# Image rows of three channels interleaved over the partitions in the patch embedding of a vision tower

## The chip, the cores and the metric

The kernel runs on one core of a Trainium2 chip. The metric is the device time of one execution in microseconds (us). It is given as the median of several executions, and one more execution was recorded by the hardware profiler.

## The reference, cut to what matters

The input is 128 images of three channels with 224 x 224 float32 pixels. Each image is cut into 8 x 8 patches of 28 x 28 pixels. A patch, with its three channels, is a vector of 3 * 28 * 28 = 2352 numbers, and a weight of 128 x 2352 turns it into a token of 128 numbers:

```python
patches = X.reshape(B, C, N_PATCHES, PATCH, N_PATCHES, PATCH)
patches = patches.transpose(0, 2, 4, 1, 3, 5).reshape(B, N_PATCHES * N_PATCHES, IN_D)
tokens = jnp.einsum('bpi,hi->bph', patches, W) + b
```

A class token goes in front (65 tokens per image), and all are multiplied by position factors. Then come a gated attention block with a damped moving average over each image position's 128 images, its layer norms, and a mixture of 8 experts of which each takes the 1024 tokens with the highest router scores, works on them, and adds its weighted result into the output. All of it is float32.

## The kernel before, in words

Names: B = 128 images, C = 3 channels, PATCH = 28, NP = 8 patches per row of patches, ROWS = C * PATCH = 84, EXTRA = 42, KROWS = 126, PASSES = 19, CHUNK = 16 images, RING = 3.

**Loading.** The images are loaded in 64 chunks. Chunk n holds, for 16 images, the 28 pixel rows of one row of patches, in all three channels. It goes into one of three ring buffers `RAW` with pixel rows on the partitions: `load_chunk` (L418) issues on the SP queue one DMA per channel, 28 partitions x 16 images x 224 pixels (896 bytes in one piece). In the kernel before, `raw` puts channel c on the partitions 28c to 28c + 27, so that the row p of channel c stands on partition 28c + p. `stage_W` on SP issues the load of chunk n + 3 when chunk n has left its ring buffer.

**Spreading.** The sum over 2352 products is made as 19 passes of a matmul over up to 126 partitions: a pass takes one pixel column q of the patch on the partitions 0 to 83, and for the last REST = 9 columns the pixel rows are also put on the partitions 84 to 125, so that two passes share the work of one more column. ScalarE copies the first 19 columns of each chunk out of the ring buffer (`stage_C` on ACT, L794, three pieces). GpSimd copies the other 9 columns into a staging tile `ST` (`stage_C` on POOL, L563), and two DMAs on its own queue (`stage_w`, L576, here called the extras) bring the partitions 0 to 41 and 42 to 83 of it to the partitions 84 to 125 of the operand.

**Weights.** The weight `WN`, 128 outputs x 2352, is put by three copies on VectorE (L863 to L865) into `WP`, which has for each pass t the 126 or 84 weights in the order in which the pixel rows stand on the partitions. TensorE transposes it (L1315 to L1319) and ScalarE brings it to `WT`.

**Order of the work.** One list, `SLOT`, sets for all engines the order of the stages within half a row of patches: "C k piece", "w k" and "W k" are the copy, the extras and the next load of chunk k of four, and the other letters are the stages of two groups of four tokens each, the newer (a) and the older (b). Every engine runs its own stages in this order. TensorE puts the token passes (`token_pass`, L1333) between the stages. A pass of a half row begins once all four of its chunks have been copied and their extras have landed. The group's matmul L1399 (stage D) comes once in each half row and waits for ScalarE's L710 (stage F), which in ScalarE's order stands behind copies of chunks. In the iteration for i = 0 there is only the class token's small group; the full groups begin in the iteration for i = 1.

After the last token pass the last groups are finished, the experts' tokens are chosen, gathered, worked on and scattered. The change does not touch that part.

Of the kernel before, what the change touches and what calls it, by code (L numbers as in the profile page):

```python
# [35 lines left out]
def vit_tower(nc, x, tok_w, tok_b, cls_token, pos_embed, proj_v_w, proj_v_b, proj_mx_w, proj_mx_b,  # L36
# [10 lines left out]
    B, C, IMG, _ = x.shape  # L47
    SEQ, D = pos_embed.shape
    NP = 8
    PATCH = IMG // NP  # L50
# [3 lines left out]
    HEADS = damping.shape[1]  # L54
    MAXPOS = (rel_pos_w.shape[0] + 1) // 2
    E, _, FF = w1.shape
    FC = FF // 128
    CAP = 1024
# [14 lines left out]
    ROWS = C * PATCH  # L73
    EXTRA = ROWS // 2
    KROWS = ROWS + EXTRA
    REST = 9
    PASSES = PATCH - REST
    HALF = B // 2
    NCOL = HALF * NP
    CHUNK = 16  # L80
# [5 lines left out]
    RING = 3  # L86

    ctx = ExitStack()
    with ctx:
# [13 lines left out]
        RAW = flat[:, 2 * PLANEW + STAGEW:2 * PLANEW + STAGEW + RING * RAWW].rearrange("p (a n) -> p a n", a=RING)  # L103
# [50 lines left out]
        WN = slab1[:, 0:C * PATCH * PATCH]  # L154
        WP = slab1[:, 2352:2352 + PASSES * 128].rearrange("p (t k) -> p t k", t=PASSES)
# [193 lines left out]
        def group(row, u):  # L349
            g = 2 * row + 1 + u  # L350
            return Group(row, g, u, 4, 4 * g - 3, 1 - u)
# [30 lines left out]
        def run(eng, stages, tokens_at=None, last=True):  # L382

            def iteration(i, slots, tokens, more):
                for u, (a, b) in enumerate(slots):
                    for s, w in slot(i, u, a, b, tokens, more):
                        if s in stages:
                            stages[s](*w)
                        if tokens_at and tokens and s not in "KCWw":
                            tokens_at(s, i, a, u)  # L390
                    if tokens_at and tokens:
                        tokens_at("end", i, a, u)

            def pair(i):
                return (group(i - 1, 0), group(i - 2, 1)), (group(i - 1, 1), group(i - 1, 0))
            iteration(0, ((CLS, None), (None, None)), True, True)
            iteration(1, ((group(0, 0), CLS), (group(0, 1), group(0, 0))), True, True)
            for i in range(2, NP - 1):
                iteration(i, pair(i), True, True)
            iteration(NP - 1, pair(NP - 1), True, False)  # L400
            if last:
                iteration(NP, pair(NP), False, False)
                iteration(NP, ((None, group(NP - 1, 1)),), False, False)


        @block.sync
        def _(sp):
            def rows_of(k, hy, c):
                return x[CHUNK * k:CHUNK * k + CHUNK, c, ds(hy * PATCH, PATCH), :].rearrange("b p w -> p b w")

            def raw(n, c):
                return RAW[PATCH * c:PATCH * c + PATCH, n % RING, :].rearrange("p (b w) -> p b w", b=CHUNK)

            def load_chunk(n):

                if n < CHUNKS * NP:
                    for c in range(C):
                        sp.dma_start(raw(n, c), rows_of(n % CHUNKS, n // CHUNKS, c)).then_inc(load[n % RING].sem, 16)  # L418

            def stage_W(k, hy):  # L420

                n = CHUNKS * hy + k
                sp.wait_ge(*copied.done(n))
                sp.wait_ge(*staged.done(n))
                sp.sem_inc(passed_sp.sem, 1)
                load_chunk(n + RING)

            load_chunk(0)
            sp.dma_start(WN, tok_w).then_inc(w_loaded.sem, 16)
            for n in range(1, RING):  # L430
                load_chunk(n)
            for k in range(4):
                stage_W(k, 0)

            def stage_M(gr):
                sp.wait_ge(*dve_M.done(gr.g, 3))
                sp.dma_start(out[:, ds(gr.position, gr.tiles), :], O[:, 0:gr.tiles, :]).then_inc(out_stored.sem, 16)

            def stage_R(gr):
                sp.wait_ge(*dve_Q.done(gr.g))  # L440
                sp.sem_inc(passed_sp.sem, 1)
                sp.dma_start(rows_v[:, ds(gr.position, gr.tiles), 0:D], XR[:, 0:gr.tiles, :]).then_inc(row_stored.sem, 16)

            run(sp, {"W": stage_W, "M": stage_M, "R": stage_R}, last=False)


            def load_experts(h, e):
                sp.dma_start(W1s[:, h, :], w1[ds(e, 1), :, :].rearrange("e d f -> d (e f)")).then_inc(w_in[h].sem, 16)
                sp.dma_start(W2s[:, h, :, :], w2[ds(e, 1), :, :].rearrange("e (c f) d -> f (e c) d", f=128))\
                    .then_inc(w_in[h].sem, 16)  # L450

            sp.wait_ge(*pe_tok[0].done(NP - 1))
            sp.wait_ge(*pe_tok[1].done(NP - 1))
            for h in range(2):
                load_experts(h, h)
            for gr in (group(NP - 2, 1), group(NP - 1, 0), group(NP - 1, 1)):
                stage_M(gr)
                stage_R(gr)


            sp.wait_ge(*pr_ready.done(0))
            sp.dma_start(rows_v[:, :, D:ROW], PR).then_inc(pr_stored.sem, 16)

            for e in range(1, E - 1):
                sp.wait_ge(*pe_y.done(2 * e - 1))
                load_experts(1 - e % 2, e + 1)

            sp.wait_ge(*out_stored.done(LAST))
            sp.wait_ge(*row_stored.done(LAST))
            sp.wait_ge(*pr_stored.done(0))  # L470
# [379 lines left out]
        def _(dve):  # L850
# [8 lines left out]

            dve.wait_ge(*c_loaded.done(0))  # L860
            dve.wait_ge(*w_loaded.done(0))
            wn = WN.rearrange("p (k q) -> p q k", q=PATCH)
            dve.tensor_copy(WP[:, :, 0:ROWS], wn[:, 0:PASSES, :])  # L863
            dve.tensor_copy(WP[:, 0:REST, ROWS:KROWS], wn[:, PASSES:PATCH, 0:EXTRA])
            last = dve.tensor_copy(WP[:, REST:2 * REST, ROWS:KROWS], wn[:, PASSES:PATCH, EXTRA:ROWS])  # L865
            last.then_inc(wp_ready.sem, 1)


# [236 lines left out]
            for it in range(STEPS):  # L1105
                k = it % 7
# [5 lines left out]
                for j in range(2):  # L1112
                    last = dve.tensor_scalar(seen[0:KEYS, j, :], keys[0:KEYS, :], CA[:, j:j + 1], 0.0, ALU.is_lt, ALU.add,
                                             accum_out=cnt[0:KEYS, j:j + 1])
# [497 lines left out]
```

## Time and profile before

| | us |
|---|---|
| median of 3 executions | 1035.58 |
| lowest and highest | 1031.78, 1038.38 |
| the profiled execution, its own time | 1028.54 |
| its span in the trace | 1026.8 |

The trace counts from the span's start. PE is TensorE's matmul, PEld its weight load, DVE is VectorE, ACT is ScalarE, POOL is GpSimd, SP is the engine that only issues DMAs; SPq is its queue. A group of instructions is named by its line and by what it writes and reads; XS is the large tile that holds ring buffers, staging tile and operand alike. "DMA share" is the mean busy share of the core's 16 DMA engines.

### The profile page before, as it was taken

The page shows a single profiled execution, that of the slowest core. Times are in us where ns is not written, and L with a number is a line of the kernel's source. Part 1 is how long each engine was busy: PE and PEld are TensorE (multiplying, and loading weights), DVE is VectorE, ACT ScalarE, POOL GpSimd, SP SyncE. Part 2 cuts the span into 40 slices and gives each one's busy share as a digit, 9 for nine tenths or more (in the row PEclk, how much of TensorE's full clock was granted, in tenths as well). Part 3 has the DMA queues.
Part 4 walks back from the last instruction along what each step waited for, and adds up shares of the span by engine and source line. Part 5 has one row for each costly group of instructions (what it writes and reads, how often), then busy time and mean ns, then how long its engine had stood idle before and what let it go on. Part 6 is the DMA issues. An engine that isn't in the chain of part 4 may idle for free.

```text
span 1026.8 us, 9698 instructions
## 1 busy us (share of the span) xinstructions
PE 739.8 (72%) x2872; PEld 396.3 (39%) x2872; DVE 552.4 (54%) x1238; ACT 446.5 (43%) x729; POOL 474.5 (46%) x486
## 2 busy tenths in 40 slices
PE   0268379979998999999989995625214599996740
PEld 0123135435444544554445454404113455553310
DVE  0210156676778578877876777692687534321110
ACT  0634346647656656665666532321261233322200
POOL 2232344454545445554554422261200658888775
PEclk9778789989999999999999997866555699988875
DMA  9799999998999999999999301000010123444332
GB/s 218 145 190 190 183 189 183 186 196 179 201 183 190 204 202 194 204 211 204 177 204 201 82 21 42 20 11 11 21 11 1 45 57 60 81 63 66 36 32 25
DMA packets 135648, 126.31 MB, mean 123 GB/s; under 512 B 17589, under 2 KB 125997, under 8 KB 135469
## 3 DMA queue, kind: packets, MB, share of 16 engines
q1 hardware_dynamic: 113600, 91.27, 43.5%
q0 software_dynamic: 19456, 33.44, 18.0%
q10 hardware_dynamic: 2540, 0.99, 0.5%
q8 instruction: 23, 0.38, 0.2%
q14 instruction: 29, 0.23, 0.1%
HBM read 87.92 MB, written 12.98 MB: 98 GB/s over the span
## 4 chain that ended last, share of the span: by engine, by line
PE 30%; DMA 22%; POOL 15%; DVE 11%; issue 9%; ACT 7%; SPq 3%; ACTq 1%; POOLq 0%; DVEq 0%
DMA XS<-in_x 18%; PE bank L1333 12%; POOL out L617 9%; POOL XS L606 4%; ACT XS L794 3%; SPq L418 3%; ACT XS L812 2%; PE bank L1399 2%; DVE XR L892 2%; PE bank L1431 2%; PE bank L1416 2%; PE bank L1462 2%; PE bank L1402 1%; DVE Y L950 1%; DMA out<-XS 1%
## 5 line engine op out<-in xcount | busy, mean ns | idle before, releaser
L1333 PE MATMUL bank<-XS,WT 126*128 126x512 f32 (+1 forms) x608 | 314.2, 653 | 38.3 <-DMA XS<-XS 38.3
L794 ACT ACTIVATE XS<-XS 84x1152 f32<-84x1152 f32 (+1 forms) x192 | 188.9, 1027 | 71.0 <-DMA XS<-in_x 69.6
L1333 PEld LDWEIGHTS bank<-XS,WT 126*128 126x128 f32 (+1 forms) x608 | 113.9, 196 | 175.9 <-issue 175.1
L563 POOL COPY XS<-XS 84x1152 f32<-84x1152 f32 x64 | 89.3, 1395 | 104.1 <-DMA XS<-in_x 100.5
L617 POOL DMA_INDIRECT out<-XS x64 | 101.3, 1583 | 24.8 <-issue 18.6
L606 POOL DMA_INDIRECT XS<-token_rows,XS x64 | 65.2, 1019 | 77.2 <-issue 65.4
L576 POOL DMA_DIRECT2D XS<-XS x128 | 71.4, 560 | 63.2 <-PE bank L1333 48.3
L950 DVE TENSOR_TENSOR_SCAN Y<-qdec,XT 128x512 f32<-128x512 f32 (+1 forms) x68 | 77.4, 1159 | 7.5 <-ACT XT L681 7.5
L837 ACT ACTIVATE XS<-bank,VT 128x512 f32<-128x512 f32 x64 | 44.0, 687 | 65.5 <-PE bank L1539 65.5
L1539 PE MATMUL bank<-XS 128*128 128x512 f32 x128 | 66.3, 666 | 1.1 <-ACT XS L681 0.8
L956 DVE SCALAR_TENSOR_TENSOR ET<-Y,ema_c,ET 128x512 f32<-128x512 f32 (+1 forms) x68 | 63.5, 933 | 1.8
L1549 PE MATMUL bank<-XS 128*128 128x512 f32 x128 | 57.5, 592 | 0.0
L1399 PE MATMUL bank<-ET,WmT 128*128 128x512 f32 (+1 forms) x34 | 23.7, 786 | 42.5 <-ACT ET L710 42.4
L539 POOL TENSOR_TENSOR QT<-QT,XT 128x512 f32<-128x512 f32 (+1 forms) x17 | 23.6, 1391 | 61.1 <-ACT QT L762 61.1
L912 DVE SCALAR_TENSOR_TENSOR tokT<-bank,VT 128x512 f32<-128x512 f32 x16 | 17.7, 1109 | 61.3 <-PE bank L1333 61.3
L681 ACT ACTIVATE XS<-bank 128x512 f32<-128x512 f32 x16 | 9.6, 597 | 83.1 <-PE bank L1530 83.1
L1243 DVE TENSOR_SCALAR XS<-bank,VT 128x512 f32<-128x512 f32 x16 | 12.0, 749 | 62.1 <-PE bank L1549 62.1
L892 DVE TENSOR_SCALAR XR<-O,mvC,rsC 128x128 f32<-128x128 f32 x65 | 38.5, 855 | 12.4 <-POOL rsC L489 12.4
L487 POOL TENSOR_SCALAR rsB<-mvB 128x4 f32<-128x4 f32 (+1 forms) x17 | 15.1, 889 | 61.2 <-DVE mvB L905 61.2
L1011 DVE SCALAR_TENSOR_TENSOR G<-bank,VT,GT 128x512 f32<-128x512 f32 (+1 forms) x34 | 24.5, 727 | 33.8 <-PE bank L1431 33.3
L986 DVE TENSOR_TENSOR S<-bank,relb 128x512 f32<-128x512 f32 (+1 forms) x17 | 11.3, 667 | 57.3 <-PE bank L1416 57.3
L1253 DVE TENSOR_TENSOR XS<-bank,XS 128x512 f32<-128x512 f32 x16 | 11.1, 692 | 53.3 <-DMA out<-XS 46.5
(229 smaller groups left out, 1293.2 us busy)
## 6 DMA issues: line engine op xcount, KB each, us to landing
XS<-in_x SPq DMA_DIRECT2D x192, 392.0 KB
XS<-XS POOLq DMA_DIRECT2D x128, 189.0 KB, 8.8
out<-O SPq DMA_DIRECT2D x16, 256.0 KB, 10.9
token_rows<-XR SPq DMA_DIRECT2D x16, 256.0 KB, 12.4
XS<-in_L_ffn_W SPq DMA_DIRECT2D x16, 256.0 KB, 3.2
XS<-in_L_tok_W SPq DMA_DIRECT2D x1, 1176.0 KB, 10.3
XS<-token_rows,XS POOLq DMA_INDIRECT x64
out<-XS POOLq DMA_INDIRECT x64
```

The costliest lines, as they stand in the source:

```text
L563: pool.tensor_copy(ST[0:ROWS, n % 2, :, :, :].rearrange("p m j r -> p m r j"), px[:, :, :, PASSES:PATCH])\
L576: pool.dma_start(area(slice(ROWS, KROWS), k // 4, a, m0, m0 + CCOL // 2), ST[EXTRA * a:EXTRA * a + EXTRA, n % 2, :, :, :]).then_inc(extras ...
L606: pool.indirect_dma_start(out=XG[h][:, k, :], out_offset=None, in_=rows_d, in_offset=bass.IndirectOffsetOnAxis(ap=IDX[:, e, k:k + 1], axis ...
L617: pool.indirect_dma_start(out=out_flat, in_=OW[:, e % 2, k, :], in_offset=None, out_offset=bass.IndirectOffsetOnAxis(ap=IDX[:, e, k:k + 1] ...
L794: ins = act.activation(area(slice(0, ROWS), k // 4, piece, m0, m0 + CCOL // 2).rearrange("p m j r -> p m r j"), px[:, :, :, REST * piece:m ...
L892: last = dve.tensor_scalar(dst(t), src(t), mv[:, gr.parity, t, 0:1], rs[:, gr.parity, t:t + 1], ALU.subtract, ALU.mult)
L950: dve.tensor_tensor_scan(Y[:, h % 2, 0:n], qdec[:, h, 0:n], XT[:, p, 0:n], 0.0, ALU.mult, ALU.add)\
L956: dve.scalar_tensor_tensor(out=ET[:, gr.parity, 0:n], in0=Y[:, h % 2, 0:n], scalar=ema_c[:, h:h + 1], in1=ET[:, gr.parity, 0:n], op0=ALU.m ...
L1333: ins = pe.matmul(TOK[half][:, :], WT[rows, t, :], area(rows, half, t // REST)[:, :, t % REST, :], start=(t == 0), stop=(t == PASSES - 1))
L1399: pe.matmul(DB0[:, 0:n], WmT[:, 1, :], et, start=True, stop=True).then_inc(pe_D.sem, 1)
L1539: pe.matmul(bank[3 + f][:, :], W1s[:, h, 128 * f:128 * f + 128], XGT[:, half, :], start=True, stop=True).then_inc(pe_hid.sem, 1)
L1549: last = pe.matmul(bank[7][:, :], W2s[:, h, f, :], HT[:, half, f, :], start=(f == 0), stop=(f == FC - 1))
```

## The change

The rows of the three channels are interleaved over the partitions: row p of channel c stands on partition 3p + c in place of 28c + p. Each load DMA still has 28 partitions, but they are three apart and reach from c to c + 81. The three weight copies write the weights in the same order. The staging tile, the extras, the copies out of the ring and the matmuls keep their shapes and partitions; what they hold is in another order.

```diff
             def raw(n, c):
-                return RAW[PATCH * c:PATCH * c + PATCH, n % RING, :].rearrange("p (b w) -> p b w", b=CHUNK)
+                return RAW[c:ROWS:C, n % RING, :].rearrange("p (b w) -> p b w", b=CHUNK)
...
             dve.wait_ge(*w_loaded.done(0))
-            wn = WN.rearrange("p (k q) -> p q k", q=PATCH)
-            dve.tensor_copy(WP[:, :, 0:ROWS], wn[:, 0:PASSES, :])
-            dve.tensor_copy(WP[:, 0:REST, ROWS:KROWS], wn[:, PASSES:PATCH, 0:EXTRA])
-            last = dve.tensor_copy(WP[:, REST:2 * REST, ROWS:KROWS], wn[:, PASSES:PATCH, EXTRA:ROWS])
+            wn = WN.rearrange("o (c p q) -> o q p c", c=C, q=PATCH)
+            part = PATCH // 2
+
+            def rows(t0, t1, k0, k1):
+                return WP[:, t0:t1, k0:k1].rearrange("o t (p c) -> o t p c", c=C)
+
+            dve.tensor_copy(rows(0, PASSES, 0, ROWS), wn[:, 0:PASSES, :, :])
+            dve.tensor_copy(rows(0, REST, ROWS, KROWS), wn[:, PASSES:PATCH, 0:part, :])
+            last = dve.tensor_copy(rows(REST, 2 * REST, ROWS, KROWS), wn[:, PASSES:PATCH, part:PATCH, :])
             last.then_inc(wp_ready.sem, 1)
```

## Rows read from the trace of the kernel before

**Rows 1.** The page's part 2, DMA: busy tenths and GB/s in 40 slices.

```profile
DMA  9799999998999999999999301000010123444332
GB/s 218 145 190 190 183 189 183 186 196 179 201 183 190 204 202 194 204 211 204 177 204 201 82 21 42 20 11 11 21 11 1 45 57 60 81 63 66 36 32 25
```

**Rows 2.** The page's part 6, DMA issues, count and size of one.

```profile
XS<-in_x SPq DMA_DIRECT2D x192, 392.0 KB
XS<-XS POOLq DMA_DIRECT2D x128, 189.0 KB, 8.8
out<-O SPq DMA_DIRECT2D x16, 256.0 KB, 10.9
```

**Rows 3.** Timeline of POOL: the staging copy of chunks 2, 3, 4, 11, 15.

```profile
30.31 1.29 POOL L563 COPY XS<-XS 84x1152 f32<-84x1152 f32 x1 [4.69 <-DMA XS<-in_x]
46.83 1.28 POOL L563 COPY XS<-XS 84x1152 f32<-84x1152 f32 x1 [13.17 <-DMA XS<-in_x]
53.03 1.29 POOL L563 COPY XS<-XS 84x1152 f32<-84x1152 f32 x1 [3.62 <-issue]
...
112.91 1.28 POOL L563 COPY XS<-XS 84x1152 f32<-84x1152 f32 x1 [5.84 <-DMA XS<-in_x]
...
146.85 1.29 POOL L563 COPY XS<-XS 84x1152 f32<-84x1152 f32 x1 [2.38 <-DMA XS<-in_x]
```

**Rows 4.** The chain that ended last, three of its pieces from 27 to 150 us.

```profile
14.91 12.75 DMA lnb<-in_L_attn_ln_b
...
39.10 7.48 DMA XS<-in_x
...
114.98 9.64 DMA XS<-XS
```

**Rows 5.** Timeline of PE: the group's matmul L1399, one per half row.

```profile
149.66 2.07 PE L1399 MATMUL bank<-ET,WmT 128*128 128x512 f32 x2 [5.86 <-ACT ET L710]
...
401.22 1.13 PE L1399 MATMUL bank<-ET,WmT 128*128 128x512 f32 x2 [1.49 <-ACT ET L710]
434.60 1.13 PE L1399 MATMUL bank<-ET,WmT 128*128 128x512 f32 x2 [0.40 <-ACT ET L710]
```

**Rows 6.** The chain again, L1399 of the last loading half row and of the next.

```profile
574.46 1.12 PE bank L1399 x2
...
606.63 1.13 PE bank L1399 x2
```

**Rows 7.** The table of waits, from 190 to 580 us.

```profile
ACT XS L794 <- DMA XS<-in_x: 25.8, 12, 6.9
```

**Rows 8.** Timeline, all engines: a chunk copy that waits, and L710 behind it.

```profile
398.17 2.50 ACT L794 ACTIVATE XS<-XS 84x1152 f32<-84x1152 f32 x2 [2.24 <-DMA XS<-in_x]
...
400.55 0.62 ACT L710 ACTIVATE ET<-ET 128x512 f32<-128x512 f32 x1
```

**Rows 9.** Busy time by stretch: the last two columns are DMA share and GB/s.

```profile
42.00:44.00 2.00, 0.00 (x0) 0.00 (x0) 0.00 (x0) 1.42 (x2) 0.00 (x0) 0.50 0.99 190
...
100.00:150.00 50.00, 28.21 (x75) 13.18 (x74) 16.77 (x38) 19.98 (x26) 20.29 (x26) 0.80 0.97 186
...
618.00:620.00 2.00, 0.75 (x7) 0.51 (x6) 1.61 (x4) 0.80 (x2) 0.00 (x0) 1.00 1.04 304
```

**Rows 10.** Timeline from 27 us: the three weight copies on DVE.

```profile
27.68 1.70 DVE L863 COPY XS<-XS 128x1596 f32<-128x1596 f32 x1 [27.68 <-DMA lnb<-in_L_attn_ln_b]
...
29.29 0.52 DVE L864 COPY XS<-XS 128x378 f32<-128x378 f32 x1
29.73 0.53 DVE L865 COPY XS<-XS 128x378 f32<-128x378 f32 x1
```

**Rows 11.** One line of the source, L418: the load DMAs as issued on SP.

```profile
L418 SPq DMA_DIRECT2D XS<-in_x x192: 315/566/5013, 0.8 to 561.3; - x192
```

**Rows 12.** The table of waits, from 35 to 190 us.

```profile
POOL XS L563 <- DMA XS<-in_x: 67.8, 13, 13.2
...
PE bank L1333 <- DMA XS<-XS: 38.3, 3, 22.5
```

## The prediction, made before the changed kernel was run

> **What bounds the kernel now.** I read the page's slices first. The DMA engines are 90% busy or more in nearly every slice up to the 22nd (some 565 us), and they move 180 to 210 GB/s there; after that they are mostly idle [rows 1]. So the first 565 us look like a transfer-bound stage, and the last 450 us, from the last token pass on, have other limits and hold no image load. The sizes of the DMAs give the load of a chunk: three DMAs of 392 KB, which is 1.204 MB, and two extras of 189 KB, which is 0.387 MB, in all 1.591 MB [rows 2].
>
> The timeline of POOL confirms it for the ramp. Its staging copy starts as soon as a chunk has landed. Chunk 4 is staged at 53.03 us and chunk 15 at 146.85, so 11 chunks take 93.8 us, 8.53 us each [rows 3]. 1.591 MB in 8.53 us is 187 GB/s, and the stretch from 100 to 150 us shows 186 GB/s at a DMA share of 0.97 [rows 9]. Nothing but transfers sets the pace there. In the table of waits of that stretch POOL waits 67.8 us for the loads and TensorE 38.3 us for the extras [rows 12].
>
> From 150 us on full groups are in the pipeline, and another limit stands close by. The group's matmul L1399 comes once per half row. It stands at 149.66 us and, 12 half rows later, at 574.46 [rows 5, 6]: 424.8 us, 35.4 each. One of these periods, 401.22 to 434.60, is only 33.38 us with all four chunks in it [rows 5]. The first period with no load left, 574.46 to 606.63, is 32.17 us [rows 6]. So the groups' own chain of dependences needs 32 to 33.4 us, and only the rest is the transfers' fault. A typical case: a chunk copy on ScalarE waits 2.24 us for its load, and L710, for which L1399 waits, stands right behind it [rows 8]. From 190 to 580 us these waits are 25.8 us in total [rows 7].
>
> **The change part by part.**
>
> *The loads.* The number of DMAs, their bytes and their pieces of 896 bytes stay. Only the 28 partitions that one DMA writes change: neighbours before, every third one now. What pace can a load have? From 42 to 44 us almost nothing but loads of chunk 3 is under way: 190 GB/s at a DMA share of 0.99 [rows 9]. From 618 to 620 us the same 16 engines fetch expert weights from the same memory, onto all 128 partitions, and move 304 GB/s at 1.04 [rows 9]. So an engine that is called busy does not have the same pace in both; something holds the image loads. The chunk's 1.204 MB take 6.34 us at 190 GB/s, and would take 3.96 us at 304. The two ends are a saving of 0 and of 2.4 us per chunk; an end below zero is in the rivals. I take 243 GB/s, near the middle, since the 28 partitions are spread over the tile but are still 28 and not 128: 4.95 us, a saving of 1.4 us per chunk.
>
> The row shows 190 GB/s for a load onto 28 neighbouring partitions. The Trainium skill, page "SBUF — State Buffer", section "Door 1: The DMA port swizzle (why [64,N] ≈ [32,N])", says that DMA writes pass through 16 ports of 27.2 GB/s each, that four neighbouring partitions (and the four that lie 32 further) share one, and that a span's pace follows the ports it reaches. By that rule 28 neighbours reach 7 ports, 190 GB/s, and the trace agrees exactly. Three apart they reach 13 ports, and the fullest has 8 of a chunk's 84 rows instead of 4 of each DMA's 28; the page's estimate for the new loads would be 84/8 times 27.2 = 286 GB/s, 4.2 us per chunk.
>
> *Issue on SP.* 192 issues of 0.32 us at least, 0.57 in the median [rows 11]. Their number stays. I cost the stride of three at nothing; below the load's pace it is hidden as long as three issues stay under a chunk's period, about 7 us. The long ones, up to 5.01 us [rows 11], are issues that the full queue holds back; with a faster queue they shorten.
>
> *The weight copies.* Three copies of 1.70, 0.52 and 0.53 us, which lie on the path to the first chunk copy at 35.4 us [rows 10]. They read single elements far apart before and after, and write in rows before and after. I cost the new order at 0; the ends are -0.3 and +2.7 us, the latter if the longer stride doubled all three.
>
> *Extras, chunk copies, matmuls.* Same shapes on the same partitions: 0. The extras take 0.387 MB at 190 GB/s, 2.04 us of the engines per chunk. Their own pace may change by who writes beside them; for that see the rivals.
>
> **The sum**, against the profiled execution's own 1028.5 us:
>
> (a) Start. Chunk 3 is fetched alone, 7.48 us [rows 4]: -1.4. The constants land at 27.66 us behind three chunks [rows 4], which would need 4.2 us less; the constants themselves have a share in it, so I count half: -2. Together -3.4.
>
> (b) Chunks 3 to 11, staged at 46.83 and 112.91 us [rows 3], 8 intervals: 8 x 1.4 = -11.2. This goes through to TensorE, since the second iteration's first token pass waits for the extras of chunk 11, which land at 124.6 [rows 4].
>
> (c) Those extras, 9.64 us in a shorter queue [rows 4]: -1. Chunks 12 to 15 until L1399 at 149.66: 4 x 1.4 = -5.6, of which I count -5, as L1399 itself was idle for 5.86 us before it [rows 5]. Together -6.
>
> (d) The 12 half rows from 149.66 to 574.46. The engines would need, per half row, 4 x (4.95 + 2.04) = 28.0 us, and two stores of 256 KB [rows 2] at 190 GB/s, 2.8 us: 30.8 in all. That is below the 33.4 us of the groups' chain, which now becomes the bound: 12 x (35.4 - 33.4) = -24. This agrees with the 25.8 us of waits [rows 7]. If the transfers' waits vanish wholly, 32.2 us is the floor and the term is -38; if a wait of 1 us per half row stays, it is -12.
>
> (e) From 574 us on: 0. The groups, the choice of tokens and the experts run as before.
>
> Sum: -3.4 - 11.2 - 6 - 24 = -44.6, about -45. The profiled execution would have 984 us. It lies 7 us under the median of 1035.6; I take the same difference off the median: 990.6, rounded 990. After the change the transfers are late less often, and in the steady stage what is late next is VectorE's and TensorE's chain through a group.
>
> **The rivals.**
>
> *Nearly the full pace* (chance 0.20). Once no neighbours are written by one DMA, the loads come near the 304 GB/s of the weight load [rows 9]: at 285 GB/s a chunk takes 4.2 us, 2.1 less. The page's rule on ports, above, would have it so. Then (a) is -5, (b) is -17, (c) is -7.5 (the idle time in front of L1399 limits it) and (d), with 27 us of transfers under a chain of 32.2 to 33.4, some -30: -60 in all, 976 us. For it: all loads of a chunk are in flight together, so that their rows cover the tile more evenly than one DMA does. [...]
>
> *No change* (0.17). What holds the image loads is not where they are written but how they are read: pieces of 896 bytes from rows far apart, against long rows for the expert weights [rows 9]. Then every term is 0: 1036 us. For it: the rows of before cannot tell the two apart. Against it: the extras, which read no DRAM, share the stretch at the same 187 GB/s [rows 9], so the reading of short rows cannot be all of it. A part of the same doubt: the Trainium skill, page "DMA: Bandwidth & Descriptors", section "Why a DMA increments its semaphore by 16 and not by 1", has a DMA of 28 partitions use 14 engines at most, before and after. No row here shows single engines.
>
> *Only the ramp gains* (0.06). The loads are faster, but in the steady stage the order of the slots makes each load be asked for so late that the copies wait as before; (a) to (c) stay, (d) is 0: -20.6, 1015 us. Against it: 33.38 us was reached with loads under way [rows 5].
>
> *Slower* (0.06). The extras write the partitions 84 to 125. Before, two of three load DMAs (partitions 0 to 55) wrote far from them; now every load writes from the bottom up to partition 83. If that hinders the extras, their 2.04 us per chunk grow. It decides from the point at which they lose more than the loads' 1.4 us, at 1.7 times their time. At 2.5 times, 5.1 us, a chunk needs 8.38 + 3.06 - 1.4 = 10.0 us, a half row 42.9 with its stores, 7.5 more than now, over 12 half rows +90, and +20 in the ramp: 1145 us; at 2 times it is +0.6 us per chunk, over 64 chunks +40: 1075 us, which I take for it. Against it: TensorE waited for extras only three times, all in the ramp [rows 12], and loads and extras overlap already.
>
> **How the numbers follow.** The forecast itself has 0.51, the others 0.20, 0.17, 0.06, 0.06. The forecast's own range is 975 to 1005: (d) between -12 and -38, the load's saving between 1 and 1.8 us. The range for 8 in 10 goes from 965, where all ends on the good side come together (-70), to 1030, inside the case of no change. About 1% (10 us) is what a measurement of this kernel can tell from no change. Faster by more than that: the forecast, nearly the full pace, the ramp alone, 0.77 together. Within 1%: 0.17. Slower: 0.06.
>
> **What would show it.** Right: in the ramp chunks are staged some 7.1 us apart in place of 8.53, with over 210 GB/s; L1399 comes every 33 to 34 us; the waits of chunk copies for loads between 190 us and the last load fall from 25.8 us to under 6; the DMA share in the steady stage falls from 0.97 towards 0.9; the stage from the last loading half row on is as long as before. Wrong: 8.5 us and 187 GB/s as before (no change), or 6.4 us or less (nearly the full pace). Extras that land clearly later than 8.8 us after issue [rows 2] would speak for the slower case. An L863 of much over 1.7 us would put the weight copies right in the sum. The forecast as a whole falls if the loads get faster and L1399 still comes every 35 us.

## The result, and the profile after

The changed kernel has a median of 1003.23 us in four executions (1000.45 to 1005.40). The kernel before, run beside it once more, has 1033.68 us over four. The ratio of the two is 0.970, 95% interval 0.965 to 0.975: faster by 30 us. The forecast was 990 us with a gain of 45; the time lies inside the forecast's own range, 975 to 1005 us, near its upper end, and the gain is two thirds of what was foretold.

The page of the changed kernel, its span and the parts that answer to [rows 1, 2]:

```profile
span 1001.4 us, 9698 instructions
...
DMA  9699998898889888988986120000010223443332
GB/s 218 150 206 208 201 205 197 197 217 196 206 197 217 201 202 195 217 192 203 209 195 161 37 64 21 0 22 10 11 11 4 48 58 62 83 65 64 35 34 24
...
XS<-in_x SPq DMA_DIRECT2D x192, 392.0 KB
XS<-XS POOLq DMA_DIRECT2D x128, 189.0 KB, 7.7
out<-O SPq DMA_DIRECT2D x16, 256.0 KB, 6.9
```

The same bytes move at 192 to 217 GB/s in the full slices while the loads last, where it was 177 to 211, and the engines' digits fall from 9 to 8 in many slices: the transfers have room again. Extras land 7.7 us after their issue in place of 8.8, stores after 6.9 in place of 10.9.

The timeline of POOL, the staging copies of the chunks 3, 4, 11 and 15, as in [rows 3]:

```profile
46.70 1.29 POOL L563 COPY XS<-XS 84x1152 f32<-84x1152 f32 x1 [12.45 <-DMA XS<-in_x]
52.35 1.29 POOL L563 COPY XS<-XS 84x1152 f32<-84x1152 f32 x1 [3.06 <-issue]
...
107.30 1.28 POOL L563 COPY XS<-XS 84x1152 f32<-84x1152 f32 x1 [5.36 <-DMA XS<-in_x]
...
138.65 1.30 POOL L563 COPY XS<-XS 84x1152 f32<-84x1152 f32 x1 [1.13 <-DMA XS<-in_x]
```

Chunk 4 to chunk 15 now takes 86.3 us, 7.85 per chunk; it was 8.53. The ramp is still bound by transfers, at 0.97 of the engines as before and with 203 GB/s in place of 186:

```profile
100.00:150.00 50.00, 33.44 (x80) 15.11 (x79) 17.13 (x39) 22.27 (x31) 21.10 (x27) 0.80 0.97 203
...
300.00:350.00 50.00, 47.67 (x152) 23.35 (x151) 41.68 (x83) 31.84 (x48) 26.84 (x30) 1.00 0.91 209
```

In the steady stage (the second line) the DMA share is 0.91. The group's matmul, which is L1404 in the changed kernel and was L1399 in [rows 5, 6]; timeline of PE:

```profile
141.46 2.08 PE L1404 MATMUL bank<-ET,WmT 128*128 128x512 f32 x2 [3.54 <-ACT ET L710]
...
312.09 1.13 PE L1404 MATMUL bank<-ET,WmT 128*128 128x512 f32 x2 [0.33 <-ACT ET L710]
345.94 1.12 PE L1404 MATMUL bank<-ET,WmT 128*128 128x512 f32 x2 [0.33 <-ACT ET L710]
...
550.06 1.13 PE L1404 MATMUL bank<-ET,WmT 128*128 128x512 f32 x2 [0.33 <-ACT ET L710]
```

Twelve half rows take 408.6 us, 34.05 each, and eight of them 33.85 to 33.88, with the same 0.33 us of idle time before the matmul. Such a regular beat points to a chain and not to transfers; an experiment below tests it. In the table of waits over the whole kernel the chunk copies wait 35.7 us for loads in 11 waits, in place of 69.6 in 23; in the table from 190 to 550 us there is none for a load down to 0.2 us, where before 25.8 us stood [rows 7].

```profile
POOL XS L563 <- DMA XS<-in_x: 80.9, 15, 12.4
...
ACT XS L794 <- DMA XS<-in_x: 35.7, 11, 5.2
PE bank L1338 <- DMA XS<-XS: 34.8, 3, 22.3
```

So the 25.4 us between the two spans are: 8.2 before the first full group's L1404 (149.66 to 141.46), 16.2 in the twelve half rows (424.8 to 408.6), and 1.0 in the rest, which should not change (452.3 and 451.3). The medians differ by some 5 us more than the two profiled executions, whose own times are 1028.54 and 1003.19 us.

### The profile page after: what moved, and what is told of

It reads as the page before. It is cut to its first block, busy times and chain, and to the rows that moved or that the text cites. A ratio compares the mean times of both kernels' runs of the same rounds, so it can differ in the third digit from the quotient of the medians.

```text
span 1001.4 us, 9698 instructions
## 1 busy us (share of the span) xinstructions
PE 736.4 (74%) x2872; PEld 393.2 (39%) x2872; DVE 555.0 (55%) x1238; ACT 446.7 (45%) x729; POOL 473.0 (47%) x486
## 4 chain that ended last, share of the span: by engine, by line
PE 26%; DVE 24%; POOL 20%; issue 14%; DMA 8%; ACT 5%; SPq 2%; ACTq 1%; POOLq 0%; DVEq 0%
PE bank L1338 10%; POOL out L617 9%; DMA XS<-in_x 5%; POOL XS L606 5%; DVE Y L955 4%; PE bank L1436 3%; DVE stats L905 3%; DVE O L897 2%; DVE XR L897 2%; DVE QT L1030 2%; ACT XS L812 2%; POOL rsB L489 2%; SPq L418 2%; PE bank L1421 2%; PE bank L1467 2%
## 5 line engine op out<-in xcount | busy, mean ns | idle before, releaser
L1338 PE MATMUL bank<-XS,WT 126*128 126x512 f32 (+1 forms) x608 | 313.6, 651 | 34.8 <-DMA XS<-XS 34.8
L794 ACT ACTIVATE XS<-XS 84x1152 f32<-84x1152 f32 (+1 forms) x192 | 187.9, 1028 | 37.0 <-DMA XS<-in_x 35.7
L563 POOL COPY XS<-XS 84x1152 f32<-84x1152 f32 x64 | 89.4, 1397 | 84.1 <-DMA XS<-in_x 80.9
L897 DVE TENSOR_SCALAR XR<-O,mvC,rsC 128x128 f32<-128x128 f32 x65 | 41.1, 894 | 9.8 <-POOL rsC L489 9.8
L1016 DVE SCALAR_TENSOR_TENSOR G<-bank,VT,GT 128x512 f32<-128x512 f32 (+1 forms) x34 | 24.5, 727 | 33.4 <-PE bank L1436 32.9
L897 DVE TENSOR_SCALAR O<-O,mvB,rsB 128x128 f32<-128x128 f32 x65 | 29.3, 512 | 16.1 <-POOL rsB L489 16.1
```

Source lines behind the costliest of these rows:

```text
L563: pool.tensor_copy(ST[0:ROWS, n % 2, :, :, :].rearrange("p m j r -> p m r j"), px[:, :, :, PASSES:PATCH])\
L794: ins = act.activation(area(slice(0, ROWS), k // 4, piece, m0, m0 + CCOL // 2).rearrange("p m j r -> p m r j"), px[:, :, :, REST * piece:m ...
L897: last = dve.tensor_scalar(dst(t), src(t), mv[:, gr.parity, t, 0:1], rs[:, gr.parity, t:t + 1], ALU.subtract, ALU.mult)
L1338: ins = pe.matmul(TOK[half][:, :], WT[rows, t, :], area(rows, half, t // REST)[:, :, t % REST, :], start=(t == 0), stop=(t == PASSES - 1))
```

## The experiments

The theory before the first of them: the pace of a load hangs on which partitions are written at the same time; the change bettered it a little, and in the steady stage another chain then took over. The rivals: the reading side or the engines' own pace; any distance between rows; the weight copies; and, for the steady stage, transfers that cost in spite of missing waits.

### The pace of a load by itself

A kernel with nothing but loads in seven parts, one after the other:

```diff
+            part(0, 28, [(0, 1), (28, 1), (56, 1)])
+            part(1, 28, [(0, 3), (1, 3), (2, 3)])
+            part(2, 28, [(0, 2), (1, 2), (56, 1)])
+            part(3, 16, [(0, 1), (16, 1), (32, 1)])
+            part(4, 16, [(0, 4), (1, 4), (2, 4)])
+            part(5, 16, [(32, 4), (33, 4), (34, 4)])
+            part(6, 28, [(0, 4), (1, 4), (2, 4)])
```

The numbers are the part, the rows of one DMA, and for each of three DMAs the first partition and the step.

> The loads by themselves: no compute, seven parts one after the other, each 30 DMAs of image rows (896-byte pieces, 16 images), differing only in the partitions written. Everything else of the kernel is left out. Placement theory (partitions that lie in one block of four, or 32 apart, hinder each other when two DMA engines write them at the same time; 14 engines of two rows each for 28 rows, 16 engines for 16 rows): part 1, 28 neighbours as before the change, 185 to 190 GB/s; part 2, every third, 210 to 240; part 3, every second for two channels, about as part 1 with at most 200; part 4, 16 neighbours, 100 to 125 GB/s; part 5, 16 rows four apart from partition 0 on, 190 to 215; part 6, the same 16 rows four apart but from partition 32 on, so that no two share a block, over 300 GB/s; part 7, 28 rows four apart, about 200. Rival, reading side or the engines' own pace: all parts with 28 rows run at one pace within 5%, and parts 4 to 6 within 5% of each other. Rival, only neighbourhood matters: every part but 1 and 4 runs at one pace, and parts 5 and 6 are equal.

Measured, a table of stretches, each inside one part; the last two columns are DMA share and GB/s:

```profile
10.00:60.00 50.00, 0.00 (x0) 1.00 0.99 195
70.00:118.00 48.00, 0.00 (x0) 1.00 0.98 218
130.00:185.00 55.00, 0.00 (x0) 1.00 0.99 187
195.00:240.00 45.00, 0.00 (x0) 1.00 1.16 119
255.00:282.00 27.00, 0.00 (x0) 1.00 1.14 197
290.00:307.00 17.00, 0.00 (x0) 1.00 1.03 332
315.00:360.00 45.00, 0.00 (x0) 1.00 0.99 213
```

The four parts with 28 rows read the same pieces of the same tensor, and the parts 4, 5 and 6 the first 16 rows of each. Parts 4, 5 and 6 have the same count of DMAs, rows and bytes, and 5 and 6 even the same step: only the first partition is 0 in one and 32 in the other, and the pace is 197 and 332 GB/s. So neither the reading side nor the engines' own pace nor the distance of the rows can be the cause; where the rows are written is. All seven values fall as the placement theory had them, save that neighbours got 195 where 190 was the upper end. Every second row (in two of the three DMAs), 187, is even slower than neighbours, which the rival "any distance helps" cannot explain. The DMA share is between 0.98 and 1.16 in all parts and says nothing of the pace. And 332 may be no upper end: in part 6 no issue on SP took longer than 0.61 us, while in part 5 the longest took 1.78, and 30 issues of 224 KB, 0.65 us apart, are themselves only some 354 GB/s. So in part 6 the issuing may have been what held the pace.

The Trainium skill, page "SBUF — State Buffer", section "Door 1: The DMA port swizzle (why [64,N] ≈ [32,N])", tells part 5 from part 6: its blocks of four partitions, of which the one 32 further shares a port, give part 5 eight ports and part 6 sixteen. But its rule, ports reached times 27.2 GB/s, comes near only in part 1 (estimate 190, 195 measured), part 4 (109, 119 measured) and, less well, part 5 (218, 197 measured). By it part 3, where two of three DMAs reach eight ports, should be faster than part 1 with seven, and it is slower. In part 7 the 28 rows reach all sixteen ports and get 213 GB/s, less than part 2 with thirteen; for the changed placement I had worked out an estimate of 286 from it, and 218 was measured.

Reaching many places is thus not enough. My reading is that the engines work through their rows in step, so that what counts is who writes at the same moment. It was the theory written down before the run, and the seven values fit it; but no row here shows single engines, and it stays a reading.

### Loads with the extras and stores beside them

> Loads with the extras beside them: six parts of 6 chunks each, three load DMAs and, as each chunk lands, its two DMAs from GpSimd's queue from partitions 0 to 83 onto 84 to 125; in parts 4 to 6 also a store of 256 KB per two chunks. Everything else is left out. Placements in turn: neighbours (before), every second for two channels, every third (the change). Placement theory with the pace of the loads alone (195, 184 and 217 GB/s): the second is no faster than the first, with or without stores; the third 8 to 10% faster. If the second comes out 2% or more ahead of the first here, the extras or stores profit from it, and that explains what it gained in the steady stage of the kernel.

Measured, again by stretches, the parts in their order:

```profile
5.00:45.00 40.00, 4.63 (x9) 1.00 0.97 191
60.00:100.00 40.00, 4.01 (x8) 1.00 0.97 185
115.00:150.00 35.00, 4.01 (x8) 1.00 0.97 205
165.00:205.00 40.00, 4.08 (x9) 1.00 0.98 203
220.00:262.00 42.00, 4.27 (x9) 1.00 0.98 196
278.00:315.00 37.00, 4.78 (x10) 1.00 0.97 223
```

The placements are neighbours, every second, every third. Without stores they reach 191, 185 and 205 GB/s, with stores 203, 196 and 223. The order is that of the loads alone, and the changed placement is 7 and 10% ahead of the old one. All bytes together, extras included, move faster: the slower case of the prediction is gone.

### The weight copies alone

This kernel leaves out the new placement and keeps the new order of the weights, so that its products pair the wrong rows; its work is the same.

```diff
             def raw(n, c):
-                return RAW[c:ROWS:C, n % RING, :].rearrange("p (b w) -> p b w", b=CHUNK)
+                return RAW[PATCH * c:PATCH * c + PATCH, n % RING, :].rearrange("p (b w) -> p b w", b=CHUNK)
```

> The change's weight copies alone, image rows placed as before (the products pair other rows, which costs the same time). Placement theory: the weight copies are worth nothing, 1030 to 1037 us, the ratio to before within 0.5% of 1, issues of a load on SP again from 0.32 us, chunks staged 8.5 us apart. Rival, that a part of the gain comes from the weights' side: under 1025 us.

> The weight copies alone again, on the same chip as the run above, as its yardstick in the trace: 0.996 to 1.004 of before, half rows of 35.4 to 35.9 us.

First comparison: 1045.06 us and 0.996 of before, interval 0.991 to 1.001, on a chip where before too had 1047.5; second, with more rounds: 1028.16 us and 0.9997, interval 0.996 to 1.003. Worth nothing, as expected. In the changed kernel the large copy takes 1.65 us, where [rows 10] had 1.70:

```profile
27.31 1.65 DVE L868 COPY XS<-XS 128x1596 f32<-128x1596 f32 x1 [27.31 <-DMA lnb<-in_L_attn_ln_b]
```

The whole gain is thus that of the line `raw`.

### Every second partition

```diff
             def raw(n, c):
-                return RAW[c:ROWS:C, n % RING, :].rearrange("p (b w) -> p b w", b=CHUNK)
+                at = slice(c, 2 * PATCH, 2) if c < 2 else slice(2 * PATCH, ROWS)
+                return RAW[at, n % RING, :].rearrange("p (b w) -> p b w", b=CHUNK)
```

with the weights in the matching order, in five copies.

> Channels 0 and 1 interleaved (2p + c), channel 2 left on partitions 56 to 83, weights in the matching order with two more copies. By the block rule 12 of 14 engines still meet another one in channels 0 and 1 and all in channel 2, so placement theory expects at most a quarter of the gain: 1022 to 1036 us, chunks staged 8.2 to 8.5 us apart. Rival, any distance between the rows helps: two thirds of the gain, about 1013 us, chunks 8.05 us apart. Issues on SP: if distance makes them dear, two of three cost 0.8 us, else 0.3.

> The every-second placement again, since its first comparison (0.984 of before) does not fit the loads measured by themselves, where it was the slowest of the three. If those decide: 0.993 to 1.003 of before, half rows of 35 us or more, chunks 8.5 us apart in the ramp. If the first comparison holds, 0.98 to 0.99 and something in the steady stage profits that neither set of bare loads contained.

The first comparison gave 0.984 (interval 0.976 to 0.992), more than placement theory had allowed; but the executions of before scattered there from 1040 to 1062 us. The second, on another chip with nine executions, gave 1021.81 us, 0.993 (0.990 to 0.996). In the ramp the chunks come 8.5 us apart, as without any change of placement. In the steady stage twelve half rows take 418.0 us, 34.8 each; the run of the weight copies alone on the same chip has 425.8, 35.5 each. So "any distance helps" is refuted for the ramp and for bare loads. Over the whole kernel 0.7% of the change's 3% is there, by the interval 0.4 to 1.0%. But all of it lies in the steady stage, and there it is not small: 7.8 us of twelve half rows (425.8 to 418.0), where the change itself has 16.2. What it comes from, while bare loads in this placement are slower, is open; it is not the extras or the stores as the mixed kernel had them. So in the steady stage something about a placement counts besides the pace of bare loads.

### What the transfers are still worth

The changed kernel with 4 of 16 images in each load from chunk 3 on; the ring buffers keep older rows for the others.

```diff
-                        sp.dma_start(raw(n, c), rows_of(n % CHUNKS, n // CHUNKS, c)).then_inc(load[n % RING].sem, 16)
+                        m = CHUNK if n < RING else CHUNK // 4
+                        sp.dma_start(raw(n, c)[:, 0:m, :], rows_of(n % CHUNKS, n // CHUNKS, c)[:, 0:m, :])\
+                            .then_inc(load[n % RING].sem, 16)
```

> The changed kernel, but from chunk 3 on each load DMA brings 4 of its 16 images, the rest of the ring buffer keeps older rows. It tells what transfers are still worth. If the group's chain alone sets the steady stage, its half row stays at 33.9 us there, and only the ramp gets shorter, by some 30 us: about 970 us. Rival, transfers still cost in the steady stage in spite of the missing waits: the half row falls to 33 us or less and the time to 960 or less.

It took 981.21 us in one execution, where about 970 was expected. On this chip before had 1047.5 us, and what follows the twelfth half row is longer in its traces whatever the kernel: 465.7 us here and 464.2 in the weight copies alone, in place of 451 to 452. So the stretches of the trace are the better witness. Stretches, and the group's matmul (L1406 here):

```profile
300.00:350.00 50.00, 47.64 (x148) 22.57 (x147) 41.25 (x88) 32.20 (x48) 27.32 (x31) 1.00 0.35 99
```

```profile
309.51 1.13 PE L1406 MATMUL bank<-ET,WmT 128*128 128x512 f32 x2 [0.33 <-ACT ET L712]
343.39 1.12 PE L1406 MATMUL bank<-ET,WmT 128*128 128x512 f32 x2 [0.34 <-ACT ET L712]
```

The DMA share falls from 0.91 to 0.35, and the half row stays at 33.88 us (twelve of them take 406.0 us, 33.83 each, against 34.05). In the changed kernel's steady stage transfers cost next to nothing any more; the rival is out. Only the ramp gets shorter: its first full group comes at 107.7 us in place of 141.5, so there 34 us are still the transfers'.

### What sets the 33.86 us

The forecast had 33.4, and [rows 6] showed 32.17 without loads. In the changed kernel one of GpSimd's staging copies and one of VectorE's instructions stand like this in the timeline, once per half row:

```profile
244.51 1.26 POOL L563 COPY XS<-XS 84x1152 f32<-84x1152 f32 x1
...
244.57 2.03 DVE L897 TENSOR_SCALAR O<-O,mvB,rsB 128x128 f32<-128x128 f32 x4 [0.94 <-POOL rsB L489]
```

The four tiles of L897 take 2.03 us beside the copy; before, in a half row without copies, the same four took 1.12 us (606.85 us in its trace). How this comes about shows at the sister instruction that writes XR, first in the quarter loads with a copy beside it, then in the kernel before without one (timelines, cut so that only the first of the four tiles stands in the line):

```profile
316.19 1.28 POOL L565 COPY XS<-XS 84x1152 f32<-84x1152 f32 x1
316.25 1.30 DVE L899 TENSOR_SCALAR XR<-O,mvC,rsC 128x128 f32<-128x128 f32 x1 [0.42 <-POOL rsC L491]
```

```profile
581.18 0.35 DVE L892 TENSOR_SCALAR XR<-O,mvC,rsC 128x128 f32<-128x128 f32 x1 [0.42 <-POOL rsC L489]
```

The first tile, 0.35 us by itself, takes 1.30 and ends 0.08 us after the copy. So VectorE gets on only when GpSimd's copy is over. The Trainium skill, page "SBUF — State Buffer", section "Who interferes with whom", says that VectorE and GpSimd share a pair of ports which one holds for a whole instruction. The trace agrees, by the 1.30 us above.

The experiment: on top of the quarter loads, the staging copy moves one column in place of nine.

```diff
-                pool.tensor_copy(ST[0:ROWS, n % 2, :, :, :].rearrange("p m j r -> p m r j"), px[:, :, :, PASSES:PATCH])\
+                j = REST if n < 2 else 1
+                pool.tensor_copy(ST[0:ROWS, n % 2, :, 0:j, :].rearrange("p m j r -> p m r j"),
+                                 px[:, :, :, PASSES:PASSES + j])\
```

> The changed kernel with a quarter of each load (as in the quarter-loads run) and, from chunk 2 on, GpSimd's staging copy of one column instead of nine. The steady stage there was 33.86 us per half row with no wait for a load. If the chain is longer than the 32.17 us of the load-free half row because staging copies hold up VectorE's instructions, the half row falls to 32.0 to 32.6 us. If ScalarE's copies or the order of the stages do it, it stays at 33.9.

The group's matmul (L1408 here) and the same VectorE instruction (L901):

```profile
297.66 1.12 PE L1408 MATMUL bank<-ET,WmT 128*128 128x512 f32 x2 [0.33 <-ACT ET L714]
330.12 1.12 PE L1408 MATMUL bank<-ET,WmT 128*128 128x512 f32 x2 [0.34 <-ACT ET L714]
```

```profile
297.88 1.27 DVE L901 TENSOR_SCALAR O<-O,mvB,rsB 128x128 f32<-128x128 f32 x4 [0.94 <-POOL rsB L491]
```

32.46 us per half row, 1.4 less than with full copies, and L901 at 1.27 us. Three groups of VectorE's instructions that stand beside copies get shorter: this one from 2.04 us (in the quarter loads) to 1.27, the one that writes XR from 2.05 to 1.24, and the one that writes QT (L1032 there, L1034 here) from 1.80 to 0.95. So the staging copies lengthen the chain from 32.5 to 33.9 us, by running into VectorE's work.

A rival is that the shorter copies merely free GpSimd, whose own operations are in the chain too. Its operation ahead of L901, in the quarter loads and then here:

```profile
340.98 0.93 POOL L489 TENSOR_SCALAR rsB<-mvB 128x4 f32<-128x4 f32 x1 [3.37 <-DVE mvB L912]
```

```profile
327.71 0.93 POOL L489 TENSOR_SCALAR rsB<-mvB 128x4 f32<-128x4 f32 x1 [3.38 <-DVE mvB L914]
```

GpSimd has long been idle when VectorE's result comes, in both; its copies do not hold it up.

The three groups lose 2.4 us together and the half row only 1.4, since another bound comes first. Busy time of one half row: the quarter loads, the small staging copies, and the load-free half row of the kernel before [rows 6]:

```profile
309.51:343.39 33.88, 32.51 (x112) 16.48 (x113) 26.84 (x57) 22.29 (x35) 17.77 (x21) 1.00 0.35 98
```

```profile
297.66:330.12 32.46, 32.12 (x112) 16.56 (x112) 24.40 (x57) 22.29 (x35) 14.22 (x21) 1.00 0.37 102
```

```profile
574.46:606.63 32.17, 32.07 (x112) 16.66 (x112) 24.77 (x57) 11.50 (x24) 10.14 (x12) 1.00 0.10 29
```

The first number behind the length is TensorE's matmuls: 32.12 of 32.46 us, and 32.07 of 32.17. As the profile counts it, the floor of 32.2 us is thus TensorE's own work, and the groups' chain with its collisions lies 1.7 us above it.

### Three tries to use this

Two of the four copies of a half row moved ahead of the GpSimd operation on which VectorE waits, once in the changed kernel and once in the kernel before, with the changed kernel again as yardstick:

```diff
-                "E a", "O b", "C 1 3", "C 1 0", "w 1", "A a", "C 1 1", "H b", "V a", "C 1 2", "W 1", "C 2 0", "J b", "C 2 3",
-                "w 2", "C 2 1", "L b", "C 2 2", "W 2", "C 3 0", "c a", "Y b", "C 3 3", "w 3", "C 3 1", "d a", "F a", "M b",
+                "E a", "O b", "C 1 3", "C 1 0", "w 1", "A a", "C 1 1", "C 2 3", "H b", "V a", "C 1 2", "W 1", "C 2 0", "J b",
+                "w 2", "C 2 1", "L b", "C 2 2", "W 2", "C 3 0", "c a", "C 3 3", "Y b", "w 3", "C 3 1", "d a", "F a", "M b",
```

> The changed kernel once more, as the yardstick on this chip: ratio to before 0.965 to 0.975, half rows of 33.9 us in the steady stage, chunks staged 7.85 us apart in the ramp.

> The changed kernel with two of GpSimd's four staging copies per half row moved ahead of the GpSimd operation after which VectorE starts (C 2 3 before H b, C 3 3 before Y b). If these copies lengthen the chain by running into VectorE's instructions, the half row falls from 33.9 to 32.3 to 33.2 us and the time by 8 to 18 us against the changed kernel. Rival, the chain takes no harm from them, or the moved copies now wait for their loads: no change or slower.

> The kernel before with the same two moves. If its steady stage is bound by transfers (35.4 us), shortening the chain brings nothing: within 0.5% of before. Rival, the chain was the bound before as well: 8 us or more faster.

The changed kernel: 1002.33 us, 0.980 of before (0.974 to 0.986), half rows of 34.06. Before was faster on this chip, 1027.4 us; so the ratio is not 0.97 everywhere. With the moved copies: 1002.44 us, 0.980 (0.974 to 0.985), half rows of 33.96. No gain in the time, where 8 to 18 us were expected: the collisions went elsewhere. Two of VectorE's scans, otherwise 2.33 us, now stand beside the copy with 3.35:

```profile
261.01 3.35 DVE L955 TENSOR_TENSOR_SCAN Y<-qdec,XT 128x512 f32<-128x512 f32 x2
```

In the kernel before, the same moves make it slower, 1.007 (1.004 to 1.011), outside the 0.5% expected. The earlier copies wait for loads that are not there yet, 168.5 us in place of 100.5 in its table of waits:

```profile
POOL XS L563 <- DMA XS<-in_x: 168.5, 38, 13.2
```

In the changed kernel the same moves raise that wait only from 80.9 to 94.5 us. That fits loads that come late before the change and in time after it. It is no proof of what bound the kernel before, since the moves gained nothing where the chain was the bound either. Nor does the trace show where the 0.7% lies: it is of the fastest of ten executions, and its twelve half rows take 423.0 us (149.93 to 572.93), no more than before.

The third try gives the staging copies from chunk 4 on to ScalarE.

```diff
+                if piece == C:
+                    act.wait_ge(*load[n % RING].done(n // RING))
+                    act.wait_ge(*extras[n % 2].done(n // 2 - 1))
...
+                    act.activation(ST[0:ROWS, n % 2, :, :, :].rearrange("p m j r -> p m r j"),
+                                   px[:, :, :, PASSES:PATCH], ACT.Copy).then_inc(staged_a.sem, 1)
```

> The changed kernel with the staging copies from chunk 4 on made by ScalarE in place of GpSimd, at the same places of the order. No copy then runs into VectorE's instructions, so by the collision theory the half row falls from 33.9 towards 32.5 us, about 12 to 16 us less in all, if ScalarE has room for 5.3 us more per half row. Rival, ScalarE's order now delays the copies and L710 behind them: the half row grows to 35 us or more and the change's gain is lost.

1000.77 us (997.76 to 1002.05), 0.970 of before (0.964 to 0.977), in another comparison than the yardstick, in the trace 33.9 us per half row. The three groups of VectorE's take 1.12, 1.11 and 0.69 us there, so the collisions are gone. But ScalarE is busy 26.55 us of a half row in place of 22.32, and the chain now runs through its copies: what VectorE gains, ScalarE's longer order gives back. Against the changed kernel's 1002 to 1003 us the difference is too small to be told. None of the three tries beats it clearly, and a placement with more pace than 218 GB/s was not tried in the kernel.

## Why the prediction was right, and where it was off

**The mechanism** held. The loads got faster, the ramp stayed bound by transfers, the steady stage changed its bound from transfers to the groups' chain, the waits of the chunk copies there went, and the last 450 us stayed. All sizes but that last one were taken too large: chunks come 7.85 us apart and not 7.1, at 203 GB/s and not over 210. That the time still fell into the range, 2 us below its upper end, is in part luck. The saving per chunk, 0.68 us, lies outside the 1 to 1.8 for which the range was made; and by the same 7 us between profile and median the range is 968 to 998 for the profiled execution, which took 1003.19. The median came inside because its gain is some 5 us larger than that of the two traces, which nothing here explains.

**The pace of the changed loads** is the term that was mis-sized. I took 243 GB/s, near the middle between 190 and the 304 of the expert weights, and 1.4 us less per chunk. Measured by itself it is 218 against 195, which would be 0.65 us less per chunk, and in the kernel it is 0.68. So (b), 8 intervals, gave 5.5 us (66.1 to 60.6) in place of 11.2, and (c) gave 2.6 (36.75 to 34.16 from chunk 11 to the first full group) in place of 6. The end that I called far, 304, was no mistake: sixteen rows on distinct places do reach 332. The mistake was to think that 28 rows three apart come halfway.

**(a) The start** gave 0.1 us at chunk 3 in place of 3.4. The constants landed at 27.3 in place of 27.7 us, where 2 us had been forecast. And the issue, which I cost at nothing, took 1.2 us back. The queue's shortest issue rose from 0.32 to 0.81 us [rows 11]; the three of chunk 3 took 2.43 us in place of 1.22, which shows where a chunk is fetched alone:

```profile
L418 SPq DMA_DIRECT2D XS<-in_x x192: 809/811/4599, 0.8 to 536.4; - x192
```

Everywhere else it is hidden, as three issues take 2.4 of the 7.85 us of a chunk.

That is one pair of traces. In the others chunk 3 is staged at 46.52, 46.70 and 47.85 us with neighbours (the weight copies alone twice, and before with moved copies) and at 45.18, 45.20 and 45.58 with rows three apart (the changed kernel again and its two variants), and the constants land at 27.3 to 28.6 and at 25.8 to 26.1 us. So (a) was taken too large but is not nothing, 1 to 2.7 us in those; why the constants land when they do is open.

**(d) The steady stage** gave 16.2 us in place of 24. The bound of the chain is 33.86 us and not 33.4. The one short period of [rows 5] was no fair sample: it followed a half row with a wait for a load, and by my reading some of the work had been done in that wait, which no run tests. The load-free half row, 32.17, which the prediction read as the groups' chain, was no sample of it either: one copy stands at its start, the others are gone, and TensorE's matmuls fill it (32.07 us). What the runs showed in its place is 32.5 us with hardly any collision, and 1.4 us more with the full staging copies. The agreement with the 25.8 us of waits [rows 7], which I took as a check, was chance: all those waits went, and only 16.2 us came of it.

**The rivals.** "Nearly the full pace" is refuted for this placement, though the pace exists. "No change" and "slower" are out; the extras even land earlier. "Only the ramp gains" is out: the larger part came from the steady stage.

## What to carry to other kernels

A DMA engine's busy share near 1 does not say that it moves what it can: divide bytes by time, and compare with another load of the same kernel. Which partitions a load writes can be worth a factor of 1.7 at the same bytes and the same count of pieces, and the count of places reached by the whole transfer does not tell it; measure a few placements by themselves, in one kernel with nothing else, before one is built in. And before a stage's gain is summed, take the next bound from a stretch with all of its other work in it, not from its best period.

## What the runs showed of the hardware that was not expected

- Sixteen rows four partitions apart load at 197 GB/s from partition 0 on and at 332 from partition 32 on.
- Twenty-eight rows on every second partition (187 GB/s) are slower than neighbours (195); four apart (213) are no better than three apart (218).
- A load of 28 rows whose partitions are three apart takes SP at least 0.81 us to issue in place of 0.32, and no less with a quarter of the bytes. Four apart it is the same 0.81; with 16 rows four apart the least was 0.55 and 0.60, and with 16 neighbours 0.32. With every second partition for two of three DMAs the least of all was 0.58. Why is open.
- While GpSimd's copy of 1.28 us ran, one VectorE instruction of 0.35 us took 1.30.
